# Attention groups of a four-layer kernel in a new order on PE, DVE and ACT, with the second key projection in another PSUM bank

## The reference, cut to what matters

```
x = x * s1;  x = (x - mean(x)) * rsqrt(var(x) + eps)        # styled, then normed
q, k = (x @ Wq.T) * q_dc, (x @ Wk.T) * k_dc
v = (x @ Wv.T) * v_dc * s2
attn = softmax(q @ k.T * scale)                             # per batch and head, 64 x 64
out = (attn @ v) @ Ww.T * w_dc + (v @ Uu.T) * u_dc
x = x + out
```

## Time and profile before

| | us |
|---|---|
| median of 3 runs | 1966.09 |
| lowest, highest | 1964.46, 1973.52 |
| profiled execution, its own time | 1968.33 |
| span of its instructions | 1966.5 |

### The profile page before, as it was taken

The page is one execution under the profiler, slowest core; times in us unless marked ns, Lnnn a source line. Parts: engine busy times, 40 slices in busy tenths (PEclk is TensorE's granted clock), DMA queues, the critical chain, the costliest instruction groups (busy, mean ns, idle before and its releaser), DMA issues.

```text
span 1966.5 us, 46115 instructions
## 1 busy us (share of the span) xinstructions
PE 1763.8 (90%) x15152; PEld 821.6 (42%) x15152; DVE 1648.4 (84%) x2380; ACT 1310.0 (67%) x2166; POOL 657.6 (33%) x591
## 2 busy tenths in 40 slices
PE   7899899899898998988998997999988899899988
PEld 5555555555554455532222222445544222222244
DVE  4777877878866898989999997659989899999965
ACT  4545445545543887788998994038877899899910
POOL 0232223233223011434755561001114366566400
PEclk9999999999998999989999999999999999999999
DMA  3000000000000234454554655903443544456567
GB/s 150 2 1 0 1 1 3 27 1 0 0 1 12 104 124 167 143 170 137 170 160 125 238 162 177 296 33 125 159 150 140 176 145 152 142 184 216 153 221 272
DMA packets 127179, 228.29 MB, mean 116 GB/s; under 512 B 36084, under 2 KB 61812, under 8 KB 118004
## 3 DMA queue, kind: packets, MB, share of 16 engines
q1 hardware_dynamic: 127064, 226.80, 35.1%
HBM read 143.40 MB, written 83.36 MB: 115 GB/s over the span
## 4 chain that ended last, share of the span: by engine, by line
PE 44%; DVE 24%; ACT 14%; issue 9%; DMA 5%; SPq 3%; DVEq 1%; ACTq 0%
PE PS L912 8%; PE PS L1307 8%; PE PS L1290 8%; PE PS L1126 7%; ACT R L897 6%; DVE acc L1575 5%; DVE q L1721 4%; DMA yt<-y_d 3%; ACT ex L658 3%; DVE ex L1424 3%; PE PS L1357 2%; PE PS L1310 2%; PE PS L978 2%; DVE sm L1430 2%; DVE mx L1420 2%
## 5 line engine op out<-in xcount | busy, mean ns | idle before, releaser
L897 ACT ACTIVATE R<-q,Ast 128x512 f32<-128x512 f32 x1024 | 638.0, 709 | 48.2 <-DVE q L1721 31.6
L1721 DVE SCALAR_TENSOR_TENSOR q<-R,PS 128x512 f32<-128x512 f32 x1008 | 610.1, 675 | 22.4 <-PE PS L1290 11.5
L549 POOL TENSOR_TENSOR Uw<-Ub,rowmask 96x512 bf16<-96x512 bf16 x256 | 339.0, 1357 | 193.9 <-PE PS L1290 181.1
L1290 PE MATMUL PS<-xq,Uw 97*128 97x512 bf16 x1024 | 325.9, 395 | 57.6 <-DVE q L1721 40.3
L1307 PE MATMUL PS<-q,Wy 128*32 128x512 f32 x2016 | 283.8, 617 | 0.8 <-DVE q L1721 0.7
L1126 PE MATMUL PS<-X,Win 128*128 (+1 forms) x512 | 242.5, 615 | 5.8 <-DVEq L1554 3.0
L1290 PEld LDWEIGHTS PS<-xq,Uw 97*128 97x128 bf16 x1024 | 85.9, 98 | 372.3 <-DVE q L1721 319.0
L540 POOL TENSOR_TENSOR xlo<-xr,xmi 128x512 bf16<-128x512 f32 x64 | 73.3, 1166 | 457.9 <-ACT xmi L796 457.9
L912 PE MATMUL PS<-xn,Wl 128*128 128x512 f32 x384 | 183.9, 610 | 26.8 <-DVE xm L1400 19.0
L506 POOL TENSOR_TENSOR ex<-ex,rs 128x1024 f32<-128x1024 f32 x32 | 94.1, 2942 | 206.1 <-DVE rs L1433 206.1
L654 ACT ACTIVATE pT<-PS 128x512 f32<-128x512 f32 x128 | 75.3, 597 | 119.0 <-PE PS L978 118.9
(11 more groups left out here) (147 smaller groups left out, 2637.2 us busy)
## 6 DMA issues: line engine op xcount, KB each, us to landing
xq<-xpart_d SPq DMA_DIRECT2D x384, 192.0 KB
sg_d<-sg SPq DMA_DIRECT2D x16, 1024.0 KB, 4.0
xn_d<-z SPq DMA_DIRECT2D x16, 1024.0 KB, 4.1
y_d<-ys SPq DMA_DIRECT2D x64, 256.0 KB, 3.8
xnp<-xn_d SPq DMA_DIRECT2D x16, 1024.0 KB, 5.4
sgp<-sg_d SPq DMA_DIRECT2D x16, 1024.0 KB, 7.8
yt<-y_d SPq DMA_DIRECT2D x32, 512.0 KB, 9.8
xpart_d<-xh SPq DMA_DIRECT2D x16, 512.0 KB, 2.9
```

The source lines that it names most:

```text
L549: pl.tensor_tensor(Uw[0:XROWS, h, w, :, :, :], Ub[0:XROWS, w, 0:N, ds(s0, CH)].rearrange("p n t -> p t n").unsqueeze(2).broadcast_to([XROW ...
L897: act.activation(R[:, w, :], q[:, t % 2, w, :], ACT.Relu, scale=Ast[:, h, w, t:t + 1], bias=CLIP).then_inc(ac_r, 1)
L1290: pe.matmul(PS[:, w, :], Uw[0:KROWS, h, w, t, :, :].rearrange("p b n -> p (b n)"), xq[0:KROWS, hb, w, s8 % XT, :], start=True, stop=True). ...
L1721: v.scalar_tensor_tensor(out=q[:, s8 % 2, w, :], in0=R[:, w, :], scalar=2 * CLIP, in1=PS[:, w, :], op0=ALU.min, op1=ALU.subtract).then_inc ...
```

## The change

- **PSUM.** The keys' second half goes to bank 4 (`key_bank = (6, 4)`), no longer 7.
- **PE.** The two halves of the w projection are apart, the second behind two of the value turns; `scores(1)` comes after all value turns; `mean_sums` comes before `turn(0)`; the first key projection comes after `turn(1)`, the second after `turn(3)` and `weigh(1)`; `mean_spread`, `weigh(2)`, and the queries follow; `square_sums` comes between the u projections; `weigh(3)` after them; `rstd_spread` after `turn(4)`; `turn(6)` and `turn(7)` before the four last weighs.
- **DVE.** `residual_att` comes after `below_largest(1)`; `sums(1)` is split, and a half of the queries goes between reciprocal and early probabilities; `out_of(0)` comes after `normed`.
- **ACT.** `mean` comes before the four copies; `keys` is split, one half before the second exponent and one behind it, and then the squares.
- **Prologue.** The same bank; the queries wait for the first half's keys alone.

The diff, cut to its core:

```diff
+        key_bank = (6, 4)
@@ ACT
-            def keys(n):
-                for c in range(HC):
-                    act.wait_ge(k_mm, n * 2 + c + 1)
-                    for e in range(2):
-                        act.activation(kz[:, c, e, :], PS[:, 6 + c, :], ACT.Copy, scale=par[e]).then_inc(k_r, 1)
+            def keys(n, c):
+                act.wait_ge(k_mm, n * 2 + c + 1)
+                for e in range(2):
+                    act.activation(kz[:, c, e, :], PS[:, key_bank[c], :], ACT.Copy, scale=par[e]).then_inc(k_r, 1)
...
-                turned(it, 0)
-                turned(it, 1)
                 if two:
                     mean(it + 2, 6)
-                turned(it, 2)
-                turned(it, 3)
+                for k in range(4):
+                    turned(it, k)
+                if one:
+                    keys(it + 1, 0)
                 exponent(it, 1)
+                if one:
+                    keys(it + 1, 1)
                 if two:
                     squares(it + 2)
-                if one:
-                    keys(it + 1)
-                if two:
                     deviation(it + 2, 6)
@@ PE, body
                 if before is not None:
-                    outward_att(it - 1, before)
+                    outward_att(it - 1, before, 0)
                 pe.wait_ge(v_r, it * 2 + 2)
                 turn_values(it, 0)
                 turn_values(it, 1)
-                if before is None:
+                if before is not None:
+                    outward_att(it - 1, before, 1)
+                else:
                     dcoef(1, range(2), 4, 7)
-                pe.wait_ge(sub_r, it * 2 + 1)
-                scores(it, 1)
                 for b2 in (2, 3):
                     pe.wait_ge(vbd_r, it * 8 + 2 * b2 - 2)
                     turn_values(it, b2)
+                pe.wait_ge(sub_r, it * 2 + 1)
+                scores(it, 1)
+                pe.wait_ge(vbd_r, it * 8 + 8)
+                if two:
+                    mean_sums(it + 2, 6)
...
                 turn(it, 1)
-                pe.wait_ge(vbd_r, it * 8 + 8)
-                if two:
-                    mean_sums(it + 2, 6)
-                weigh(it, 0)
-                pe.wait_ge(pn_r, it * 2 + 1)
-                turn(it, 2)
-                weigh(it, 1)
-                turn(it, 3)
-                weigh(it, 2)
-                weigh(it, 3)
-                if two:
-                    mean_spread(it + 2, 7)
                 if one is not None:
                     pe.wait_ge(xn_r, it + 2)
+                    if two:
+                        pe.wait_ge(lmu_r, it + 3)
                     project(one, 1, 0, x1, 6, k_mm)
+                pe.wait_ge(pn_r, it * 2 + 1)
+                pe.wait_ge(pt_r, it * 8 + 1)
+                turn(it, 2)
+                weigh(it, 0)
+                pe.wait_ge(pt_r, it * 8 + 2)
+                turn(it, 3)
+                weigh(it, 1)
+                if one is not None:
+                    pe.wait_ge(pt_r, it * 8 + 3)
+                    project(one, 1, 1, x1, 4, k_mm)
+                if two:
+                    pe.wait_ge(pt_r, it * 8 + 4)
+                    mean_spread(it + 2, 7)
+                weigh(it, 2)
+                if one is not None:
+                    pe.wait_ge(k_r, it * 4 + 6)
+                    project(one, 0, 0, x1, 6, q_mm)
                     if two:
                         pe.wait_ge(xm_r, it + 3)
-                    project(one, 1, 1, x1, 7, k_mm)
-                    for m in range(HC):
-                        pe.wait_ge(k_r, it * 4 + 2 * m + 6)
-                        project(one, 0, m, x1, 6 + m, q_mm)
+                    else:
+                        pe.wait_ge(pt_r, it * 8 + 4)
+                    project(one, 0, 1, x1, 7, q_mm)
+                pe.wait_ge(sub_r, it * 2 + 2)
+                pe.wait_ge(vs_r, it + 1)
+                project(l, 4, 0, vsc, 2, u_mm)
                 if two:
                     pe.wait_ge(q_r, it * 2 + 3)
                     square_sums(it + 2, 6)
-                pe.wait_ge(sub_r, it * 2 + 2)
-                pe.wait_ge(vs_r, it + 1)
-                for m in range(HC):
-                    project(l, 4, m, vsc, 2 + m, u_mm)
+                project(l, 4, 1, vsc, 3, u_mm)
+                weigh(it, 3)
+                pe.wait_ge(pe_r, it * 2 + 2)
+                if one is not None:
+                    pe.wait_ge(k_r, it * 4 + 8)
+                turn(it, 4)
                 if one is not None:
                     pe.wait_ge(q_r, it * 2 + 4)
                 if two:
                     rstd_spread(it + 2, 7)
-                pe.wait_ge(pe_r, it * 2 + 2)
-                turn(it, 4)
...
+                pe.wait_ge(pn_r, it * 2 + 2)
+                pe.wait_ge(pt_r, it * 8 + 5)
+                turn(it, 6)
+                pe.wait_ge(pt_r, it * 8 + 6)
+                turn(it, 7)
                 pe.wait_ge(av_r, it * 2 + 1)
-                weigh(it, 4)
-                pe.wait_ge(pn_r, it * 2 + 2)
-                turn(it, 6)
-                weigh(it, 5)
-                turn(it, 7)
-                weigh(it, 6)
-                weigh(it, 7)
+                for k in range(4, 8):
+                    weigh(it, k)
@@ DVE, body
                 if before:
                     weighted(it - 1, *before, 1)
-                    residual_att(it - 1, before[1])
...
                 largest(it, 1)
                 below_largest(it, 1)
-                out_of(it, l, g, 0)
+                if before:
+                    residual_att(it - 1, before[1])
                 if two is not None:
                     centred(it + 2, 7)
-                sums(it, 1)
+                sums_of(it, 1)
                 if one:
-                    queries(it + 1, *one)
+                    queries(it + 1, *one, 0)
+                early_probs(it, 1)
+                if one:
+                    queries(it + 1, *one, 1)
...
                 if two is not None:
                     normed(it + 2, par_n, 7)
+                out_of(it, l, g, 0)
```

More of the change, by code:

```diff
@@ L701, in _ @@
             dcoef_guess(0)
-            keys(0)
+            keys(0, 0)
+            keys(0, 1)
             deviation(1, 0)
@@ L992, in weigh, with outward_att @@
                 mm.then_inc(av_mm, 1)
-            def outward_att(it, l):
+            def outward_att(it, l, m):
                 pe.wait_ge(av_r, it * 2 + 2)
-                for m in range(HC):
-                    project(l, 3, m, av, turn_bank[m], w_mm)
+                project(l, 3, m, av, turn_bank[m], w_mm)
             def body(it, l, par_n, before, one, two):
@@ L1091, in _ @@
             for m in range(HC):
-                project(0, 1, m, x0, 6 + m, k_mm)
+                project(0, 1, m, x0, key_bank[m], k_mm)
             square_sums(1, 0)
+            pe.wait_ge(k_r, 2)
             for m in range(HC):
-                pe.wait_ge(k_r, 2 * m + 2)
                 project(0, 0, m, x0, 6 + m, q_mm)
@@ L1112, in _ @@
                     body(it, l, it % 2, l, (it + 1) // G if it + 1 < AT else None, it + 2 < AT)
-            outward_att(AT - 1, LAYERS - 1)
+            for m in range(HC):
+                outward_att(AT - 1, LAYERS - 1, m)
             pe.wait_ge(x_done, LAYERS * G + 1)
@@ L1410, in normed, with queries @@
                                 ALU.mult).then_inc(xn_r, 1)
-            def queries(n, l, g):
-                for c in range(HC):
-                    v.wait_ge(q_mm, n * 2 + c + 1)
-                    v.tensor_tensor(tiled(qs[:, c, :]), tiled(PS[:, 6 + c, :]), of_layer(qk_t, l * HC + c, g),
-                                    ALU.mult).then_inc(q_r, 1)
+            def queries(n, l, g, c):
+                v.wait_ge(q_mm, n * 2 + c + 1)
+                v.tensor_tensor(tiled(qs[:, c, :]), tiled(PS[:, 6 + c, :]), of_layer(qk_t, l * HC + c, g),
+                                ALU.mult).then_inc(q_r, 1)
             def largest(it, r):
@@ L1426, in below_largest, with sums_of @@
                                 mx[:, r, :].unsqueeze(2).broadcast_to([P, 32, S]), ALU.subtract).then_inc(sub_r, 1)
-            def sums(it, r):
+            def sums_of(it, r):
                 v.wait_ge(exp_r, it * 2 + r + 1)
@@ L1433, in sums, with early_probs @@
                 v.reciprocal(rs[:, r, :], sm[:, r, :]).then_inc(rcp_r, 1)
+            def early_probs(it, r):
                 v.wait_ge(rcp_r, it * 2 + r + 1)
@@ L1437, in sums @@
                                 .unsqueeze(3).broadcast_to([P, 4, 4, S]), ALU.mult).then_inc(pe_r, 1)
+            def sums(it, r):
+                sums_of(it, r)
+                early_probs(it, r)
             def out_of(it, l, g, r):
@@ L1527, in _ @@
             demodulation(0)
-            queries(0, 0, 0)
+            queries(0, 0, 0, 0)
+            queries(0, 0, 0, 1)
             inverse_dev(1, 0)
```

## The result

Median 1915.22 us (1912.51 to 1915.77, 4 runs) against 1965.84 (1964.46 to 1973.52, 4 runs): a ratio of 0.9728, 95% interval 0.9705 to 0.9751 (the two medians as they stand divide to 0.974). The profiled execution took 1915.77 us against 1968.33, 52.6 less, with a span of 1912.7 in place of 1966.5.

What follows compares the result with a forecast made beforehand. PE, with holes, was taken to bound the attention stage. Groups 1 to 13 at 32.8 us save 43.6, group 14 5.1, the last 2.7: 51.4 us, from 1968.3 to 1916.9, forecast 1915 us as median, range 1906 to 1930.

Steps and rivals of the forecast that it cites:

- PE bounds the stage, with 2.98 us of holes: Attention stage: PE busy 33.11 of 36.09 us a group, with holes of 0.33 twice, 0.41, 1.58 and 0.33.
- (b): Second key projection to bank 4, mean_spread behind it: no longer waits for centred, so the 1.58 us hole goes.
- (c): Keys split around ACT's second exponent: the 0.33 us hole before the first query goes; the later exponent's price is hidden.
- (d): Turns ahead of weighs, weigh(3) behind the u projections: fills both 0.33 us holes; new PE neighbours taken as 0.
- (e): scores(1) behind value turns, mean_sums before turn(0): attacks the 0.41 us hole; chain 9.08 level with PE's 9.0 to 9.1.
- (a): out_of(0) behind normed, residual_att behind the second subtraction on DVE: largest(1) starts 2.1 us earlier, nothing lost.
- Groups 14 and 15: Last two attention groups: 5.1 us saved in group 14, at 30.1 us, and 2.7 us in the last.
- Group 0: First attention group, 36.89 us: turn(0) waits for the second layer's tables in either order, so saving 0.
- rival 1: Softmax chain sets the pace: turn(0) or turn(5) waits 1 us a group, 13 us less saved, 1928; chance 0.19.
- ACT's queue: Second exponent, queued behind PE's turn(3) and first key projection, comes late: 26 us less saved, 1941; chance 0.05.
- a granted clock of 1.00: Clock rival: PE without rest lowers the clock; at 0.85 a group is 38.6 us, total 1998; chance 0.04.
- Theory D: Formed after the result: DVE sets the group's pace, and losing a 2.2 us residual beside POOL is what counted.

Runs made afterwards that it cites:

- u3_scores: Changed kernel with scores(1) ahead of the last two pairs of value turns and mean_sums behind turn(1) again: 1927.03 us, ratio 0.9795.
- b2_residual_alone: Kernel before the change with only residual_att moved behind the second subtraction: 1948.41 us, ratio 0.9890.
- v1_tables_spread: Changed kernel with the second layer's tables taken apart and spread over DVE holes in groups 5 and 6: 1906.58 us, ratio 0.9671.
- v2_tables_group0: Changed kernel with the second layer's tables spread over DVE holes and, in group 0 alone, scores(1) ahead of the last value turns: 1906.03 us, ratio 0.9674.
- u2_residual: Changed kernel with residual_att back ahead of the second maximum on DVE: 1919.87 us, ratio 0.9749.
- c2_copy_in_hole: Changed kernel with one unused DVE copy added per group, ahead of the next group's first maximum where DVE stands idle: 1912.65 us, ratio 0.9706.
- c1_copy_in_chain: Changed kernel with one unused DVE copy added per group, between out_of(1) and the first subtraction: 1934.39 us, ratio 0.9816.
- b1_bank_alone: Kernel before the change with only the second key projection moved to bank 4 and the centred wait moved to the second query: 1986.09 us, ratio 1.0084.

## Why the prediction was right

- **PE bounds the stage, with 2.98 us of holes.** Right in the main: the four holes are gone from groups 1 to 13 (what rows still show there is 0.82 in group 1 and 4.25 in group 5, both before value turns), and DVE's load is not what counts, since with the copy in a hole DVE is busier and the group stays at 32.20. But the chain through DVE still ends last at `turn(0)`, by about 0.1 us a group.
- **(b) and (c), the second key projection and the split keys.** Right, and the runs put 1.40 and 0.40 us on them. The bank does not pay alone: by itself it lost 0.8%, as the first query waits for key copies that stand behind ACT's squares. The split alone was not run.
- **(d), both holes of 0.33.** Right in place. The term that I set to 0, the new neighbours on PE, was mis-sized: two turns in a row take 1.03 us, four weighs 1.17, and PE's work in a group is at most 32.20 where I had 32.54, inside the 0.4 either way that I had bounded it by. That is the larger part of the difference between 32.8 forecast and 32.2 to 32.3, which makes 5.4 us over 13 groups (49.0 against 43.6).
- **(e), chain and PE level.** Right: `turn(0)` starts 0.14 us behind the early probabilities in each group, its distance when it waits, so about 0.1 us of the 0.1 to 0.2 that I left there stayed, hidden in a tail. It follows that less PE work ahead of `turn(0)` would gain nothing more: the next gain there is a shorter chain, and the copy in it showed that it has nothing to spare. I priced the move by the hole of 0.41; what it is worth is the work that it took from behind `turn(0)` (`u3_scores`).
- **(a), the residual moved.** That it costs nothing is right. Its price was wrong: I carried 2.21 us, and most of the second microsecond was POOL's. The Trainium skill (SBUF — State Buffer, Who interferes with whom) says that a VectorE instruction with two SBUF inputs and a GpSimd instruction that reads SBUF take turns at a shared pair of ports for a whole instruction, and that the order of issue decides who waits. The trace agrees: 1.22 and 2.21 for the residual, 1.23 and 2.60 for the probabilities, 1.22 and 2.83 for `styled`; the residual moved alone (`b2_residual_alone`) took 1.21. I had the first pair's row before me and did not ask why a residual of 1024 columns takes twice as long as `centred`.
- **Groups 14 and 15.** 5.5 and 2.4 against 5.1 and 2.7: near what was worked out, `turn(0)` of group 14 waits 0.56 us (I had about 0.5), and no projection there ran at the lower clock. In group 15 four turns did in part, behind a wait of 1.85: they took 3.73 us, where two take 1.09 in the same place of `v1_tables_spread`, behind the same wait. PE timeline of the changed kernel:

```profile
558.20 3.73 PE L978 MATMUL PS<-ident,ex 128*128 128x128 f32 x16 [1.85 <-DVE ex L1450]
```

- **Group 0.** I had 0 and it lost 1.3 us. Its granted clock fell from 1.00 to 0.96, behind a hole of 2.29 that the later `scores(1)` had opened (0.94 stood there before). My estimate is that 0.04 of 38.3 us below the full clock, at a level of one half, is some 3 us at that level and 1.5 us lost: the whole loss. With the hole closed again (`v2_tables_group0`) the clock still fell; with it closed in all groups (`u3_scores`) it did not. What makes it fall there stays open. A further 1.6 us were lost ahead of group 0. The changed kernel and the runs made from it start group 0 at 45.5 to 47.8, the kernel before and the two runs made from that at 45.6 to 46.4; whether the changed prologue has a part in it is not shown. PE timeline of the changed kernel behind that hole (the scores take 1.43 at the full clock):

```profile
50.24 1.97 PE L972 MATMUL PS<-ident,vTd 128*128 128x128 f32 x8 [2.29 <-ACT vbd L664]
52.13 1.89 PE L962 MATMUL PS<-kz,qs 32*64 32x128 f32 x64
```

- **Rivals.** The softmax chain did not cost the 1 us a group of rival 1, but it ends last at `turn(0)` by about 0.1, and 0.33 us more of DVE time in it cost 1.6 us a group. ACT's queue was no limit (the second exponent at 11.97, laid out at 12.3). With PE busy throughout, the plain and loop groups keep a granted clock of 1.00. It rose from 0.95 to 1.00 in group 14; it fell where PE still waits, in group 0 and in group 5 (0.95 to 0.90, behind the hole of 4.25 at the second layer's tables). Theory D, formed after the result, fell with `u2_residual` and `c2_copy_in_hole`.

49.0 + 5.5 + 2.4 - 1.3 - 1.6 = 54.0 us up to the next stage against 51.4 forecast (the span fell by 53.8): the packing made more, the start less. That 1915 met 1915.22 is in part luck: groups 1 to 14 gave 5.8 us more than the forecast's terms, groups 0 and 15 and the start 3.2 less, for reasons that have nothing to do with each other. Undone one at a time, the parts are worth 1.40, 1.29, 0.81, 0.40, 0.18 and 0.11 us a group, 4.19 in all where the change gave 3.89, so they overlap little in the new order; in the old one the residual was worth 1.19 and the bank less than nothing.

## What to carry to other kernels

Where PE is busy for nine tenths of a stage, list its holes with their releasers and follow each releaser back through its engine's queue: a bank or a move that frees PE from one wait can run it into the next, and two small holes merged into one can cost the clock. When no idle time is left, compare start-to-start distances: an instruction that always starts at the same distance behind its releaser is still waiting. Put equal small matmul groups next to each other. Before a DVE instruction with two SBUF inputs is moved, look which POOL instruction it will stand beside and which of the two starts first.

## What the runs showed of the hardware

- A DVE instruction with two inputs in SBUF and a POOL one beside it take turns, and a shift of 0.33 us, which changed who came first, cost 1.6 us a group (`c1_copy_in_chain`: 2.83 against 1.22 for `styled`). The wait shows as a longer duration, not as idle time.
- Behind a PE hole of 2.18 us two projections took 5.3 to 5.4 us in place of 3.70 in nine groups of eleven and 3.70 in the other two; behind one of 1.58 they took 3.70 in all twelve (`b1_bank_alone`). The bank alone was slower for it by 0.8%.
- The same transposes and weighs take less in one row: four weighs 1.17 us where weigh, turn, weigh, turn, weigh takes 0.36 for each weigh.
